# Four-block attention and mixture kernel: narrow score tiles over both heads, full-row maxima in the last attention, and two rewritten orders

## The reference

```
# block 0: 4 key/value heads, each for 4 query heads; rotary on q and k
logits = einsum('bqhgd,bkhd->bhgqk', qg, k) / 8;  causal;  softmax;  times v;  @ Wo + bo
# block 3: one key/value head (k = v) for all 16, and a null key that every row sees
kv  = concat([null_kv, x @ Wkv]);  sim = q . kv / 8;  causal;  softmax;  times kv;  @ Wout
```

## Time and profile before

| | |
|---|---|
| median of 3 runs | 2268.97 us (2267.01 to 2270.85) |
| the profiled execution | 2269.74 us, span 2267.9 us |
| TensorE busy | 2031.7 us, 90% of the span |
| VectorE busy | 1442.0 us, 64% |
| GpSimd busy | 1227.0 us, 54% |
| ScalarE busy | 991.3 us, 44% |
| first attention | about 66 to 570 us |
| second attention | about 763 to 1256 us |
| last attention | about 1620 to 2187 us |

### The profile page before, as it was taken

How to read it: one execution, slowest core, us unless ns; L and a number is a source line. 1 busy time by engine, 2 the same in 40 slices (tenths; PEclk the granted TensorE clock), 3 DMA queues, 4 the chain that set the end, 5 groups by cost and what they waited for, 6 DMA issues and landing times. The chain is left out here.

```text
span 2267.9 us, 32948 instructions
## 1 busy us (share of the span) xinstructions
PE 2031.7 (90%) x10378; PEld 1276.0 (56%) x10378; DVE 1442.0 (64%) x3934; ACT 991.3 (44%) x2043; POOL 1227.0 (54%) x1600
## 2 busy tenths in 40 slices
PE   5999999999785899999999889998899999888975
PEld 3555555555683555655555566876555555444544
DVE  7788787875335666666666464525567777766733
ACT  2444444444344445544544335445324444344443
POOL 1569977777352466776677200000346666688744
PEclk7999999999896899999999889999789999999987
DMA  4235221321514324433442110000212123122233
GB/s 132 74 95 144 62 65 37 74 47 42 149 49 106 71 61 103 94 80 90 98 103 62 44 34 19 1 11 14 70 38 61 48 57 75 43 79 63 57 91 100
DMA packets 126358, 155.66 MB, mean 69 GB/s; under 512 B 22136, under 2 KB 66456, under 8 KB 125928
## 3 DMA queue, kind: packets, MB, share of 16 engines
q1 hardware_dynamic: 121832, 145.43, 25.7%
q0 software_dynamic: 4352, 8.12, 1.1%
HBM read 47.84 MB, written 17.40 MB: 29 GB/s over the span
## 5 line engine op out<-in xcount | busy, mean ns | idle before, releaser
L1507 POOL TENSOR_TENSOR acc<-acc,pr 128x512 f32<-128x512 f32 (+3 forms) x768 | 677.2, 903 | 131.7 <-ACT pr L1269 107.4
L1269 ACT ACTIVATE pr<-P 128x512 f32<-128x512 f32 (+1 forms) x768 | 397.2, 567 | 403.4 <-PE P L794 395.9
L794 PE MATMUL P<-qA,kA 128*128 128x512 f32 (+2 forms) x1152 | 446.7, 396 | 33.5 <-ACT pr L1269 33.3
L794 PE MATMUL P<-pr,vt 128*64 128x512 f32 (+3 forms) x2304 | 447.5, 510 | 4.1 <-POOL pr L1485 4.1
L794 PE MATMUL P<-qB,kB 128*128 128x512 f32 (+2 forms) x1152 | 398.0, 353 | 0.0
L1485 POOL TENSOR_SCALAR_AFFINE_SELECT pr<-pr 128x256 f32<-128x256 f32 x384 | 157.4, 410 | 360.4 <-ACT pr L1269 326.4
L794 PEld LDWEIGHTS P<-qA,kA 128*128 128x128 f32 x1152 | 221.1, 192 | 185.8 <-issue 104.8
L1882 DVE TENSOR_REDUCE mx<-P 128x1 f32<-128x512 f32 x384 | 244.6, 684 | 66.1 <-PE P L794 65.8
L794 PEld LDWEIGHTS P<-pr,vt 128*64 128x64 f32 x2304 | 147.4, 140 | 218.9 <-issue 180.9
L1504 POOL TENSOR_TENSOR acc<-pr,pr 128x384 f32<-128x384 f32 x192 | 217.8, 1145 | 85.7 <-ACT pr L1269 85.3
L794 PE MATMUL P<-kB,hq 64*128 64x512 f32 (+2 forms) x576 | 229.5, 440 | 19.0 <-DVE mx L1893 12.5
(11 more groups left out here) (306 smaller groups left out, 3227.7 us busy)
## 6 DMA issues: line engine op xcount, KB each, us to landing
qA<-hq SPq DMA_DIRECT2D x384, 128.0 KB, 2.4
kA<-stage SPq DMA_DIRECT2D x168, 128.0 KB, 2.3
qB<-qB SPq DMA_DIRECT2D x96, 128.0 KB, 2.4
kB<-stage SPq DMA_DIRECT2D x84, 128.0 KB, 2.3
nr<-null_share SPq DMA_DIRECT2D x64, 128.0 KB, 2.9
yd<-in_c_zero SPq DMA_DIRECT2D x32, 128.0 KB, 2.7
w<-in_L_W SPq DMA_DIRECT2D x16, 256.0 KB, 4.4
xg<-xg SPq DMA_DIRECT2D x24, 129.0 KB
```

The source lines that it names most:

```text
L794: return P.matmul(out, lhs, rhs, start=start, stop=stop)
L1269: S.activation(a.pr[slot][:, r, 512 - wide:512], m.bank[b][:, 512 - wide:512], AF.Exp, scale=0.125).then_inc(s.free[b], 1)
L1507: G.tensor_tensor(acc[:, sl], acc[:, sl], pt[:, sl], ALU.add).then_inc(s.acc, 1)
```

## The change

1. **Narrow score tiles** of attentions 0 and 3: the two heads of a pair share their keys, so one matmul takes both heads' queries. Instead of four matmuls of 256 columns there are two of `2 * wide`: 512 columns for width 256, and 256 for width 128. The exponentials read the packed result. Attention 1 keeps its four.
2. **Maxima of the last attention over 128 rows** (`WHOLE_MAX = (3,)`): `qA` against `kA`, high and low parts of the key, one matmul for each head. They wait for the DMAs to `qA` and `kA` instead of the cast to `hq`, and the cast no longer waits for the last maximum of the chunk before the last.
3. **Eight `pr` tiles** in the last attention instead of four.
4. **New orders** for attentions 0 and 3, with the same steps and 18 `+` a job; `V` is now written by what has been scored, which gives the same tiles as before. Attention 1 keeps its order.

```diff
--- before.py
+++ after.py
@@ -168,31 +168,33 @@
 
 
 
-WHOLE_MAX = ()
+WHOLE_MAX = (3,)
+
+TILES = {0: 4, 1: 4, 3: 8}
 
 ROUNDS = ((0, 0), (0, 2), (1, 0), (1, 2), (1, 4), (1, 6))
 
 
 
 STEPS = {
-    0: ("k0 + S + q0 k0' S R1 + q0' C1 + + V",
-        "S S q0\" V + k0\"",
-        "D1 + M1 M0 S q1 S O1 V q1'",
-        "+ S q1\" + M3 + + M2 v0 k1 + C0 D0 k1' S + k1\" V",
-        "+ + M6 S M4 O0 S R0 M7 V +",
-        "M5 S + v1 M8 S M9 V +"),
+    0: ("+ k0 S + q0 k0' S R1 + q0' C1 + + V",
+        "k0\" + S V q0\" D1 S",
+        "M1 + M0 S + q1 S + q1' V O1",
+        "q1\" + + S v0 M3 + M2 + S k1 C0 k1' V + + D0 k1\" R0",
+        "S M6 M4 + S O0 M7 V",
+        "M5 M8 + S S v1 + V M9"),
     1: ("S k0 + k0' q0 S R1 q0' C1 V v0",
         "k0\" q0\" + D1 S V M2 S + + +",
         "q1 q1' + S V q1\" + M0 + S",
         "O1 S k1 + M1 M3 + + V M4 k1' S + M5 +",
         "C0 S V + + D0 R0 M7 S",
         "O0 + S M6 V v1 + k1\" S M8 M9 +"),
-    3: ("k0 + k0' q0 q0' S + + R1 C1 V + k0\" + S",
-        "q0\" S + M0 S V",
-        "S D1 + S + M2 q1 M1 + V q1'",
-        "q1\" S C0 + O1 S V D0 + +",
-        "v0 M4 S M5 k1 + k1' M3 S + V k1\"",
-        "R0 v1 M8 S + + M7 V S O0 + M6 M9 +")}
+    3: ("q0 q0' + k0 k0' S + q0\" k0\" + C1 V + D1 S",
+        "R1 + + + S S V + + M1 M0",
+        "S q1 q1' S q1\" M2 V k1 +",
+        "k1' + S k1\" C0 v0 S M3 V D0",
+        "S + M5 M4 + V + M6 O1 S v1",
+        "M7 S + + S R0 M8 M9 V + + O0")}
 
 
 def project(L, kind, b, p, c):
@@ -261,10 +263,9 @@
             elif not j and late:
                 od.extend(late.pop(0))
         elif what == "V":
-            before = (j, r - 1) if r else (j - 1, 5)
-            if before[0] >= 0:
-                cc, k0 = ROUNDS[before[1]]
-                od.extend([("pv", L, *jobs[before[0]], cc, k) for k in (k0, k0 + 1)])
+            ready = [k for k in scored if (k[0], k[1]) != (j, r)]
+            od.extend([("pv", L, *jobs[i], ROUNDS[rr][0], kt) for i, rr, kt in ready])
+            del scored[:len(ready)]
         elif what[0] == "M" and j < 15:
             highest(j + 1, n)
         elif what[0] == "q" and j < 15:
@@ -286,6 +287,7 @@
         elif what[0] == "O" and done:
             od.add("out", *done)
 
+    scored = []
     b, p = jobs[0]
     vals, later = value_items(L)
     for c in range(2):
@@ -310,12 +312,13 @@
             for what in STEPS[L][r].split():
                 if what == "S":
                     score(j, ROUNDS[r][0], ROUNDS[r][1] + tile)
+                    scored.append((j, r, ROUNDS[r][1] + tile))
                     tile += 1
                 else:
                     step(what, j, r)
         while late:
             od.extend(late.pop(0))
-    od.extend([("pv", L, *jobs[15], 1, k) for k in (6, 7)])
+    od.extend([("pv", L, *jobs[i], ROUNDS[rr][0], kt) for i, rr, kt in scored])
     od.extend([(k, L, 1, 7, 1) for k in ("close", "dsum", "div", "out") if L == 3 or k != "dsum"])
     for items in behind:
         od.extend(items)
@@ -549,7 +552,7 @@
     def attention(stack, L, first):
         a = Box()
         nk, nv = NK[L], NV[L]
-        a.pr = [sb(stack, f"pr{i}", [128, 2, 512]) for i in range(4)]
+        a.pr = [sb(stack, f"pr{i}", [128, 2, 512]) for i in range(TILES[L])]
         if L == 1:
             attention_rows(stack, a, L)
         if L == 0:
@@ -764,7 +767,7 @@
         return i % 3, i // 3
 
     def tile_slot(self, L, b, p, c, kt):
-        n = 4
+        n = TILES[L]
         i = self.parts["score", L, b, p, c, kt]
         return i % n, self.tiles[L][i - n][1:] if i >= n else None
 
@@ -886,6 +889,8 @@
                 ww = max(wide, 256)
                 w.wait_ge(s.kqz, od.nth("kqz", L))
                 w.wait_ge(s.q_low[slot], 16 * use + 16)
+                w.wait_ge(s.q_dup[slot], 64 * use + 64)
+                w.wait_ge(s.q_max[slot], 16 * use + 16)
                 for r in range(2):
                     h = kv_of(L, 2 * p + r)
                     ks = pl.heads[L, bb, h][0]
@@ -893,14 +898,18 @@
                     w.wait_ge(s.k_dup, pl.keys_there(L, bb, h, kt // 4)[0])
                     w.wait_ge(s.k_low, pl.keys_there(L, bb, h, kt // 4)[1])
                     b, uses, _ = od.bank[item][r if wide > 256 else 0]
-                    st = m.bank[b][:, 512 - ww:512] if wide > 256 else m.bank[b][:, 256 * r:256 * r + 256]
-                    w.wait_ge(s.q_dup[slot], 64 * use + 64)
-                    w.wait_ge(s.q_max[slot], 16 * use + 16)
                     w.wait_ge(s.free[b], uses)
-                    mm(st, l1.bitcast(FR), a.qA[slot][:, r, 512 - ww:512].bitcast(FR), True, False)
-                    t = mm(st, l2.bitcast(FR), a.qB[slot][:, r, 512 - ww:512].bitcast(FR), False, True)
-                    if r or wide > 256:
+                    if wide <= 256 and L != 1:
+                        st, qs = m.bank[b][:, 0:2 * wide].rearrange("p (r n) -> p r n", r=2), (slice(0, 2), slice(512 - wide, 512))
+                    else:
+                        st = m.bank[b][:, 512 - ww:512] if wide > 256 else m.bank[b][:, 256 * r:256 * r + 256]
+                        qs = r, slice(512 - ww, 512)
+                    mm(st, l1.bitcast(FR), a.qA[slot][:, qs[0], qs[1]].bitcast(FR), True, False)
+                    t = mm(st, l2.bitcast(FR), a.qB[slot][:, qs[0], qs[1]].bitcast(FR), False, True)
+                    if r or wide > 256 or L != 1:
                         t.then_inc(s.full[b], 1)
+                    if wide <= 256 and L != 1:
+                        break
             elif kind == "pv":
                 L, bb, p, c, kt = k
                 a, (slot, _) = m.A[L], pl.tile_slot(*k)
@@ -1260,8 +1269,9 @@
                     w.wait_ge(s.acc, pl.adds[old[:4] + (max(old[4], 1),)])
                 if wide <= 256:
                     w.wait_ge(s.full[b], f)
-                    S.activation(a.pr[slot][:, :, 512 - wide:512], ps[:].rearrange("p (r n) -> p r n", r=2)[:, :, 256 - wide:256],
-                                 AF.Exp, scale=0.125).then_inc(s.free[b], 1)
+                    each = 256 if L == 1 else wide
+                    src = ps[:, 0:2 * each].rearrange("p (r n) -> p r n", r=2)[:, :, each - wide:each]
+                    S.activation(a.pr[slot][:, :, 512 - wide:512], src, AF.Exp, scale=0.125).then_inc(s.free[b], 1)
                     continue
                 for r in range(2):
                     b, _, f = od.bank[item][r]
```

## The result

The changed kernel takes 2215.86 us (median of 4 runs, 2210.53 to 2218.14), the kernel before beside it 2269.91: a ratio of 0.9758, 95% interval 0.9734 to 0.9781. That is 54 us less where 67.5 were forecast; the time lies within the forecast range. The profiled execution has a span of 2216.4 us, 51.5 less than before. A second attention that was not touched took 484 us in place of 485. The rest splits like this, measured from closing to closing as in the prediction.

What follows compares the result with a forecast made beforehand. TensorE was taken as the bound, with waits in the last attention and GpSimd as floor under sendings. Last attention and start give -58.5 us, the first attention -9: -67.5 from 2269.7 us makes 2202 us, range 2172 to 2242.

Steps and rivals of the forecast that it cites:

- the stretches with bisection: Last attention, seven stretches: from 34.4 to 30.4 us each, by tiles 0.5, maxima 1.1 and waits 2.4; -28 us.
- the last attention's first stretch: A stretch of 46 us: -4 us, since VectorE's 31.73 us busy and the clock stay.
- Narrow tiles, -8 in each of two attentions: First and last attention: two matmuls of width 128 save 0.5 us a head pair, over 16 pairs 8 us each.
- Maxima over 128 rows, -18: Last attention: full-row matmuls avoid changes of shape, saving 1.1 us a head pair, 18 us over 16 (bounds 1.6 to -1.4).
- The rival of packing: Last attention: full-row groups lose 1.4 us a pair instead of gaining 1.1, giving 2242 us; chance 0.09.
- Waits in the last attention, 2.4 us a stretch: New order removes TensorE waits for `mxe`, q's low part and exponentials: 1.8 us plus hidden time, 2.4 of 3.5.
- The start, -1: A term of the sum beside the last attention's stretches: 1 us less at the start.
- The added wait for copies of q, 0.2 to 0.5 us: Last attention: maxima now wait for the DMAs to `qA`, adding 0.2 to 0.5 us a stretch, counted within remaining waits.
- Eight tiles, 0: Last attention: four more exponential tiles save at most 2.0 us on ScalarE, off the path, so 0.
- Sendings, -10.5: Last attention, three stretches with sendings: from 35.7 to 32.2 us, with GpSimd busy 31.07 as floor; -10.5 us.
- First attention, -8 and -1: First attention: -8 us from narrow tiles and -1 from its order, -9 together, since TensorE hardly waits there.
- The signs: Expected in the changed profile: stretches 30 to 31 us with bisection, 32 with sendings, 29 with neither; no `mxe` wait.

Runs made afterwards that it cites:

- e6: The kernel before with two-head narrow score tiles alone: 2258.11 us, 0.9950 of the kernel before.
- e4: The changed kernel with narrow score tiles as before, four matmuls of 256 columns, in attentions 0 and 3: 2224.8 us, 0.9799 of the kernel before.
- e1: The changed kernel with the last attention's maxima back on 64 rows: 2219.2 us, 0.9784 of the kernel before.
- e3: The changed kernel with the last attention's old order and its maxima on 64 rows: 2249.11 us, 0.9908 of the kernel before.
- e12: The changed kernel with chunk 1's turned maxima (R1) back ahead of the closing in the last attention: 2213.47 us, 0.9748 of the kernel before.
- e11: The kernel of e9 with maxima M5 and M4 apart as well: 2207.91 us, 0.9728 of the kernel before.
- e2: The changed kernel with four tiles of exponentials in the last attention instead of eight: 2213.96 us, 0.9759 of the kernel before.
- e7: The changed kernel with the last attention's 32 sendings on every third router step instead of every second: 2201.95 us, 0.9707 of the kernel before.
- e9: The kernel of e7 with a job's last pv between maxima M8 and M9 in the last attention: 2202.24 us, 0.9696 of the kernel before.
- e5: The changed kernel with the first attention's old order: 2220.61 us, 0.9779 of the kernel before.

## Why the prediction was right, and where its sizes were off

The time lies in the range, 14 us above the forecast of 2202, and the direction is right, with two of its mechanisms: narrow tiles save TensorE's time, and the last attention's order takes waits away. That it lies so near is partly luck. Too much was forecast for the stretches with bisection (9.0 us), with sendings (9.2), with neither (3.2) and for the last one (0.9); too little for the last attention's first stretch (5.9), the slow one (0.2), the first attention (1.1) and the start. Two terms of the sum failed, the full rows and the sendings, and larger gains of the orders stood in for part of them.

*Narrow tiles, -8 in each of two attentions.* 0.5 us a steady head pair is what e6 shows in both, but not every pair is steady: alone they give 11 us, not 16 (e6). Beside the rest of the change it is 0.5 in the first and 0.2 in the last attention (e4), about 9 us in all. The step did not ask what the other edits leave of it.

*Maxima over 128 rows, -18.* This term failed: e1 gives nothing. The changes of shape were counted in the old order, with score tiles around ten groups; in the new one the ten items stand in seven groups, and four of these have `pv` behind them. The doubt in the text, "some groups stand beside each other or beside `pv`", was the whole case. The rival of packing (1.4 us lost a pair) is as wrong on the other side: a direct loss of 0.87 us a stretch is met by 0.7 us saved around it. The Trainium skill, "TensorEngine Tiling (Array Packing)", section Key Properties, says that changing the tiling mode drains the engine. The trace agrees: ahead of `pv` (128*64) the full-row pair takes 0.56 us where two such matmuls take 0.46 among their like, and the 64-row pair 0.44 where the kernel before showed 0.33.

*Waits in the last attention, 2.4 us a stretch.* e1 against e3 gives 2.4 with bisection. The size was right; the parts were not. In the seven stretches with bisection of the kernel before, the trace has a single wait of TensorE for `mxe`:

```profile
PE P L794 <- ACT pr L1269: 7.7, 14, 0.9
...
PE P L794 <- DVE qB L1858: 2.5, 7, 0.4
...
PE P L881 <- ACT mx L1252: 0.2, 1, 0.2
```

The 5.0 us of the earlier trace rows stood nearly all in the other six stretches, so the 0.4 us a stretch taken from them had nothing to win in these seven. The waits for exponentials (7.6 to 3.5 us over the seven) and for the low part of q (2.4 to none) did fall from e3 to e1; all waits that the trace shows fell from 2.3 to 0.8 us a stretch. The other 0.9 of the 2.4 us have no wait of their own and stay unexplained. (The 15.9 us are over 13 stretches, not 13.3.) The wait for `mxe` went, but not because R1 moved (e12). The order's 29 us also has 6.7 us in the first stretch. The forecast had -4 there for everything, since VectorE's 31.73 us and the clock would stay. VectorE did (32.67 us), and did not hold the stretch at 42: it took 36.5, and the granted clock rose from 0.80 to 0.95. The new order gives 36.3 to 36.7 us at 0.95 in nine of eleven profiles (e4 38.4, e11 40.3), the old one 43.4 to 46.8 at 0.80 to 0.85 in three, so this is the order's doing.

*The start, -1.* Between the last attention's first two closings the time fell from 26.5 to 21.3 us, 4.8 of it by the order (e3 against e1). The part from the second attention's last closing to this, nearly all of it untouched, took 377.2 us in place of 370.6, and 370.5 to 377.3 over all profiles, which hides it.

*The added wait for copies of q, 0.2 to 0.5 us.* It does not show.

*Eight tiles, 0.* Right (e2).

*Sendings, -10.5.* This term failed too: -1.3. The floor of 31 us of GpSimd was seen, and 32.2 us taken, 1.1 above it. What failed is the overlap: with nine or ten sendings in it a stretch takes 35.5 us at 31.5 of GpSimd, 4.0 above, and the trace shows ScalarE and VectorE (9.1 and 11.1 us over the three) waiting for sendings to land before they may fill `xs` again, with TensorE behind them. The gap before, 35.9 us at 31.1, was nearer to what stays than 1.1. With six sendings it is 31.6 us at 28.1 (e7), but there the chain of waits has no GpSimd line in four of five stretches, so those are not shown to be GpSimd's limit; in e9, as long, they are most of it.

*First attention, -8 and -1.* The sum was about right (-10.1) and its parts were not: the order alone is worth 5 us (e5). A steady head pair of the kernel before looked full, and the order still took 0.7 us from it, most of it at the maxima: busy TensorE time also holds what its neighbours cost it. The narrow tiles gave less than their 8, 4.8 us (e6) to 6.6 (e4).

*The signs.* Stretches with bisection came to 31.7 us where 30 to 31 were named, with neither to 30.4 where 29, with sendings to 35.5 where 32. No wait for `mxe`, narrow tiles of two matmuls 0.12 us apart and no wait for a DMA of q came as named; steady pairs of the first attention fell by 1.2 us where 0.5 was named.

## What to carry to other kernels

Cost a change of shape, or any saving between neighbours, in the order that the change makes, not in the one it removes. Where an engine is 90% busy in a stretch and waits for others between its own instructions, take the distance that the trace shows between busy time and length as part of the floor. Background work with a limit of its own belongs spread over all the stretches that have room: one step more between the sendings gained 10 us in its stretches and 12 to 14 in the time, about as much as the narrow tiles (9), the full rows and the eight tiles together. Before a wait's total is spread over all stretches, it has to be seen in which of them it stands.

## What the runs showed of the hardware

Two 64-row matmuls of 512 columns that run side by side take 0.44 us up to a matmul of another shape, and two full-row ones 0.56 where that shape is again another: packing gains 0.12 us there, not half of the time. A sending takes 0.99 us of GpSimd (0.96 to 1.16, 64 in the changed kernel). The first attention's first stretch took 41.2 us at a granted clock of 0.88 in the changed kernel, 38.3 at 0.96 in e7 and 45.2 at 0.78 in e9, whose first attentions are the same: differences of up to 7 us in that stretch say nothing of an edit.
